# VectorE scales the turned x before ScalarE copies the turned B out of the same PSUM bank

## The reference, cut to what matters

```python
xBC = silu(causal_conv4(x @ Win_xBC.T))           # 256 columns of x, 128 of B, 128 of C
dtp = softplus(dt + dt_bias); dA = exp(dtp * A)   # 4 heads
def step(h, (dA_t, dt_t, x_t, B_t, C_t)):
    h = dA_t * h + (dt_t * x_t) outer B_t         # state 64 x 128 per head
    return h, C_t . h + D * x_t
y = rmsnorm(ys) * norm_w * silu(z) @ Wout.T
x = layernorm(x + y)
x = layernorm(x + two_of_eight_experts(x))        # gelu, 128 -> 512 -> 128
```

## Time and profile before

| | us |
|---|---|
| runs, median (three runs: 731.25, 731.27, 729.77) | 731.25 |
| profiled execution, its own time | 729.96 |
| span of the profiled execution | 728.2 |
| PE busy | 656.8 (90%) |
| DVE busy | 567.1 (78%) |
| ACT busy | 472.8 (65%) |
| POOL busy | 459.5 (63%) |

### The profile page before, as it was taken

How to read it: one execution, slowest core, us unless ns; L and a number is a source line. 1 busy time by engine, 2 the same in 40 slices (tenths; PEclk the granted TensorE clock), 3 DMA queues, 4 the chain that set the end, 5 groups by cost and what they waited for, 6 DMA issues and landing times.

```text
span 728.2 us, 19939 instructions
## 1 busy us (share of the span) xinstructions
PE 656.8 (90%) x5075; PEld 539.5 (74%) x5075; DVE 567.1 (78%) x1876; ACT 472.8 (65%) x1174; POOL 459.5 (63%) x664
## 2 busy tenths in 40 slices
PE   7978999999999999999999679999999999999910
PEld 5846756676666666756675569999999999999910
DVE  3478898999899999999999857677666666888744
ACT  3746767776777676767676527765656656677724
POOL 5022367777777776777677565767775455677754
PEclk9999999999999999999999999999999999999975
DMA  9180001101110111011101022332432223455443
GB/s 254 38 289 15 2 26 35 45 20 42 30 45 20 42 32 43 23 39 34 41 24 37 16 74 56 91 86 79 101 94 71 75 72 94 140 164 171 140 173 123
DMA packets 56543, 54.54 MB, mean 75 GB/s; under 512 B 9562, under 2 KB 45790, under 8 KB 56176
## 3 DMA queue, kind: packets, MB, share of 16 engines
q1 hardware_dynamic: 45712, 33.67, 16.9%
q0 software_dynamic: 8416, 16.93, 6.8%
q10 hardware_dynamic: 2304, 2.65, 1.0%
HBM read 31.05 MB, written 22.63 MB: 74 GB/s over the span
## 4 chain that ended last, share of the span: by engine, by line
PE 71%; DVE 9%; issue 8%; DMA 3%; POOL 3%; ACT 2%; SPq 1%; DVEq 1%; ACTq 0%; POOLq 0%
PE p L630 12%; PE pl L621 8%; PE pj L483 6%; PE p L682 4%; PE p L712 4%; PE p L621 4%; PE p L676 4%; PE p L720 3%; PE p L658 3%; PE p L691 2%; PE pj L491 2%; PE p L594 2%; PE p L580 2%; PE p L491 2%; PE pl L527 2%
## 5 line engine op out<-in xcount | busy, mean ns | idle before, releaser
L1651 POOL DMA_INDIRECT moe_rows<-xT x135 | 134.9, 999 | 79.6 <-DVE xT L1275 47.5
L1584 POOL DMA_INDIRECT sorted_rows<-pair,slot x128 | 128.6, 1004 | 32.5 <-issue 30.4
L1033 DVE SCALAR_TENSOR_TENSOR acc<-pj,conv_w_sb,acc 128x511 f32<-128x511 f32 (+2 forms) x192 | 142.3, 741 | 4.6 <-ACT acc L815 1.6
L630 PE MATMUL p<-w,xT 128*128 x1080 | 143.5, 276 | 1.6 <-ACT xT L950 1.3
L950 ACT ACTIVATE xT<-pl,b_sb 128x128 f32<-128x128 f32 x360 | 102.7, 369 | 47.5 <-PE pl L621 45.7
L630 PEld LDWEIGHTS p<-w,xT 128*128 128x128 f32 x1080 | 131.4, 192 | 2.8 <-issue 2.8
L621 PE MATMUL pl<-xT 128*128 128x128 f32 x720 | 95.1, 275 | 2.4 <-DVE xT L1263 2.4
L1271 DVE TENSOR_TENSOR xT<-p,b_sb 128x128 f32<-128x128 f32 x135 | 39.3, 291 | 64.5 <-PE p L630 60.6
L621 PEld LDWEIGHTS pl<-xT 128*128 128x128 f32 x720 | 87.5, 192 | 2.5 <-issue 2.5
L815 ACT ACTIVATE acc<-pj,conv_b_sb,conv_w_sb 128x512 f32<-128x512 f32 x64 | 49.5, 773 | 33.6 <-PE pj L483 33.6
L483 PE MATMUL pj<-xT,w_xbc 128*128 128x512 f32 x128 | 67.2, 607 | 0.0
(11 more groups left out here) (223 smaller groups left out, 1406.8 us busy)
## 6 DMA issues: line engine op xcount, KB each, us to landing
xT<-sorted_rows SPq DMA_DIRECT2D x135, 65.0 KB, 2.4
xres<-in_x SPq DMA_DIRECT2D x16, 256.0 KB, 3.0
w<-in_w SPq DMA_DIRECT2D x2, 2048.0 KB, 10.0
acc<-moe_rows SPq DMA_DIRECT2D x12, 256.0 KB, 3.8
xT<-moe_rows SPq DMA_DIRECT2D x12, 256.0 KB, 5.5
out<-sz ACTq DMA_DIRECT2D x10, 256.0 KB, 2.6
moe_rows<-xT POOLq DMA_INDIRECT x135, 2.3
sorted_rows<-pair,slot POOLq DMA_INDIRECT x128, 2.4
```

The source lines that it names most:

```text
L630: mm = pe.matmul(y_bank(j)[:, 0:P], hT[j % 4][:, f, :], w2[:, bass.ds(e, 1), f, :].rearrange("p e d -> p (e d)"), start=(f == 0), stop=(f ...
L1033: ins = dve.scalar_tensor_tensor(out=acc[:, k, j:TOKS], in0=pj[k % 2][:, 0:TOKS - j], scalar=conv_w[:, k, TAPS - 1 - j:TAPS - j], in1=acc[ ...
L1584: pool.indirect_dma_start(out=sorted_rows[:, :], out_offset=bass.IndirectOffsetOnAxis(slot[q.par][:, c, k:k + 1], 0), in_=(rowA, rowB)[k][ ...
L1651: pool.indirect_dma_start(out=moe_rows[:, :], out_offset=bass.IndirectOffsetOnAxis(xs[k][:, P:P + 1].bitcast(I32), 0), in_=ye[j % 8], in_o ...
```

## The change

It does three things. DVE no longer waits for `Btok_ready` ahead of `Xdt`: it needs only the turned rows. ACT's copy of the turned B waits for `Xdt_ready` of the same chunk where it waited for `tr_psum`, so that the order of the two readers of `p5` is turned round in chunks 0, 1 and 2. And in chunk 0 the exponential of chunk 1's exponents, with its table load, is issued ahead of the copy, where it was issued behind it; in the other chunks it stood ahead already. PE's and POOL's code is not touched: PE still waits for both `Xdt_ready` and `Btok_ready` before it overwrites `p5`.

```diff
                 for c in range(NC):
                     n = NC * s.n + c
-                    if scan and c > 0 and (c + 1 < NC or project):
+                    if scan and (c + 1 < NC or project):
                         exp_exponents(n + 1, c + 1)
                     if scan and c + 1 < NC:
-                        act.wait_ge(tr_psum, n + 1)
+                        act.wait_ge(Xdt_ready, n + 1)
                         wait(act, state_psum, (NC - 1) * s.n + c - 1)
                         act.copy(Btok[c % 2][:, :], p5[:, CC * P:(CC + 1) * P]).then_inc(Btok_ready, 1)
-                    if scan and c == 0:
-                        exp_exponents(n + 1, c + 1)
                     if not route and c == 0:
                         enter_dt(1, G0, SEQS)
...
                         dve.wait_ge(tr_psum, n + 1)
-                        if c + 1 < NC:
-                            dve.wait_ge(Btok_ready, (NC - 1) * s.n + c + 1)
                         wait(dve, Xdd_ready, (NC - 1) * s.n + max(c - 1, 0))
                         dve.tensor_tensor(heads(Xdt[c % 2][:, :]), heads(p5[:, 0:DI]),
                                           per_head(cur[s.par][:, 0, :], c), ALU.mult).then_inc(Xdt_ready, 1)
```

## The result

| | before | after |
|---|---|---|
| median of ten runs (lowest to highest), us | 730.14 (729.39 to 731.27) | 726.88 (724.77 to 729.07) |
| profiled execution, own time | 729.96 | 724.77 |
| its span | 728.2 | 723.0 |
| its granted clock, share of full speed | 0.976 | 0.979 |

The ratio of after to before is 0.9953, with an interval of 0.9942 to 0.9964: 3.4 us less, between 2.6 and 4.2. The forecast was 727.8 with "faster" at 0.74.

The account below looks back on a forecast made before the run. DVE's path to `state` in chunk 0 was taken as the bound, with PE's path 0.20 ahead of it. 13 x 0.21 + 0.52 + 2 x 0.1 = 3.45 us off the median 731.25 gave 727.8, range 725.5 to 730.9.

Parts of the forecast that it names:

- `Xdt` 0.35 earlier, the load right behind the SiLU, the copy 0.50 behind the exponential: Chunk 0: `Xdt` at 237.93, load at 237.42 without waiting, exponential 0.79 earlier, ACT's copy from 239.21 to 239.48.
- rival A: Chunk 0: the table load waits for PE's exponents, the 13 slots gain nothing, 730.7; chance 0.14.
- the drain of some 1380 ns: Extra cost at ACT's table switch; forecast took none, else copy 1.38 later, 16 us over all slots; one chance in a hundred.
- `yv` 0.35 earlier: Chunk 0, DVE's path: `yv` starts at 240.43, so DVE could take `state` at 240.76.
- POOL takes the gain of `Xdd`: Chunk 0: POOL's scatter runs until 238.79, so `Xdd` starts at 238.80 and ends hardly earlier.
- PE's exponents don't move, `state` waits for the product, 0.19 to 0.23 a slot: Chunk 0: chunk 2's exponents stay at 239.53 to 239.57, `state` at 240.88 to 240.92 instead of 241.11; 0.21 taken.
- Rival C: Chunk 0: DVE's path decides after all, the slot gains the full 0.35, 5.3 in all, 726.0; chance 0.06.
- Rival B: Chunk 0: ACT's copy later, exponents of chunk 2 near 239.9; up to 0.18 a slot slower, 733.1; chance 0.08 with drain.
- Chunks 1 and 2 of ordinary slots give nothing: PE wants the later copy over 0.9 after it lands in chunk 1; PE's projection sets chunk 2's pace; nothing gained or lost.
- Slot 15: Chunk 2, no projection: `Xdt` at 420.35 instead of 420.87, PE at 420.88 instead of 421.40; 0.52 gained into the second phase.
- Slots 0 and 1, a choice of 0.1 each: These slots have other work around them, softplus and decays; gain chosen as 0.1 each, half of the others'.
- The sum: Whole kernel: 13 x 0.21 + 0.52 + 2 x 0.1 = 3.45 us, from the median 731.25 to 727.8, 0.47% below.

Follow-up runs that it names:

- The delays: Changed kernel, chunk 0: unread 512-column ACT copy ahead of the `Btok` copy, 780.86, ratio 1.0039; unread 8-column DVE copy ahead of the statistics, 769.00, ratio 0.9951.
- the run with the exponents ahead: Changed kernel; PE's waits for `Btok` and `Xdd` in chunk 0 put behind chunk 2's exponents: 766.15, ratio 0.9899; again 765.54, ratio 0.9914.
- the two halves: New order in chunk 0 only on the changed kernel: 767.25, ratio 0.9910; new order in chunks 1 and 2 only on the kernel before: 773.36, ratio 1.0005.
- the version with `state` first: Changed kernel, chunk 0; PE issues the product of `Btok` and `Xdd` ahead of the exponents, DVE takes `state` ahead of `yv`: 770.39, ratio 0.9962.

## Why the prediction was right, and where it was not

- **`Xdt` 0.35 earlier, the load right behind the SiLU, the copy 0.50 behind the exponential.** Right to 0.01. The load started at 234.24, 0.01 behind the SiLU and ahead of the end of PE's exponents (233.99 + 0.38 = 234.37); rival A needed it at or behind that end, and is false. The exponential starts 0.01 behind the end of the load: the drain of some 1380 ns in the Trainium skill (ScalarE: Activation LUTs, What ACT_TABLE_LOAD costs) isn't there, its 1283 ns are.
- **`yv` 0.35 earlier.** It was 0.41. The forecast read DVE's path as free of gaps and saw the exponential only as a danger for later; it already held the mask for about 0.06. At `state` this makes no difference, for PE's path decides there.
- **POOL takes the gain of `Xdd`.** Right: `Xdd` starts 235.65, right behind the scatter (234.66 + 0.96 = 235.62).
- **PE's exponents don't move, `state` waits for the product, 0.19 to 0.23 a slot.** Right: 0.20, and no more because PE now waits for ACT's copy. The delays (0.50 paid in full on ACT, 0.07 hidden on DVE) and the exponents moved ahead on the changed kernel (0.15 gained) show that PE's wait for ACT is the limit now. That DVE's path was the limit before is read from the earlier trace rows, `state` 0.33 behind `yv` without a wait; the same move on the old kernel gave nothing, but shortened PE's path too little to decide it. Rival C, all of 0.35 by this change alone, is false: that needs PE's order changed too, as in the run with the exponents ahead.
- **Rival B** did not come about; its place is the right one, its point of decision was not reached (the copy was at 1.33, as worked out). Its sum doesn't come out either: 239.57 and the added 0.08 and 2 x 0.04 make 239.73, not 239.9, and so fall short of the 239.76 that it names itself.
- **Chunks 1 and 2 of ordinary slots give nothing.** Shown by the two halves.
- **Slot 15: the step that failed.** The forecast had 0.52 pass "straight through to the second phase". The slot, chunk 2, after:
```profile
414.61 0.27 PE L654 MATMUL p<-ident,xc 128*128 128x128 f32 x1
...
414.92 0.42 DVE L1309 TENSOR_TENSOR Xdt<-p,cur 128x256 f32<-128x256 f32 x1 [1.83 <-PE p L654]
...
415.14 1.08 POOL L1580 DMA_INDIRECT sorted_rows<-pair,slot  x1 [0.22 <-issue]
...
415.45 0.66 PE L676 MATMUL p<-M,Xdt 128*64 128x128 f32 x8
...
416.25 0.63 POOL L1593 TENSOR_TENSOR Xdd<-Xdt,cur 128x256 f32<-128x256 f32 x1
...
417.02 0.67 PE L691 MATMUL p<-Xdd,Btok 128*128 128x256 f32 x2 [0.27 <-POOL Xdd L1593]
...
419.34 0.66 PE L676 MATMUL p<-M,Xdt 128*64 128x128 f32 x8
```
And before, the rows that stand beside them and the earlier trace rows:
```profile
421.39 0.60 POOL L1597 TENSOR_TENSOR Xdd<-Xdt,cur 128x256 f32<-128x256 f32 x1 [0.57 <-DVE Xdt L1313]
...
424.78 0.66 PE L676 MATMUL p<-M,Xdt 128*64 128x128 f32 x8
```
The first half came: `Xdt` 0.04 behind the turn and PE 0.57 behind it, where it was 1.09. But a scatter of POOL runs from 415.14 to 416.22. Before, POOL had been idle for 0.57 when `Xdt` released `Xdd`; now `Xdd` waits for POOL, and the product for `Xdd`, 0.27. From the end of the turn to PE's products of chunk 3 it is 4.46 after (419.34 - 414.88) and 4.47 before: all is given back. I had asked this question of POOL in chunk 0 and not here.

The runs on the other chips bear it out. Counted from slot 15's `state` of chunk 0, and taking the kernel before and the changed one on chip 8, `Xdt` of chunk 2 starts at 7.62 and 7.10 and PE's products with `M` at 8.14 and 7.62, but `Xdd` at 8.43 and 8.44, behind the scatter in both (7.32 + 1.08 = 8.40), and PE's products of chunk 3 at 11.52 in both. With the new order in chunk 0 only these products are at 8.14 and 11.52, with it in chunks 1 and 2 only at 7.62 and 11.51: the 0.52 appears with the order of chunk 2 and is gone by chunk 3. That POOL's scatter is what takes it is read from the rows; no run moved the scatter.
- **Slots 0 and 1, a choice of 0.1 each.** 0.15 in slot 0; slot 1 can't be parted from the clock.
- **The sum.** 2.62 measured where 13 x 0.21 = 2.73 stood, and about 0.25 for slots 0 and 1, make 2.9 on the first chip; the forecast had 3.45, of which 0.52 did not exist. The measured 3.4 (2.6 to 4.2) doesn't tell the two apart, the traces do. The number itself, 727.8, came out 0.9 above the 726.88 measured because it stood on the median of three runs, 731.25; the ten runs give 730.14, and the same sum taken from there gives 726.7.

Open: the second phase. From the GELU's load to the end it took 332.6 to 335.4 us in the four profiles of chip 8, whose code for it is the same: about as much as the whole effect. In the traces of these chips ACT waits there for something that the profile calls remote, 41 to 54 us in all; in the first two profiles it doesn't. The ratio of 0.9910 for the order in chunk 0 only, with a first phase like the changed kernel's, is not explained; its profiled execution, 771.74, was the longest of the seven, so no trace shows a short one.

## What to carry to other kernels

Where two paths join, write down both ends: the gain of shortening one is the distance to the other (0.20 of 0.41 here), and the move that shortens the second (a wait put behind work that doesn't need it) gave 0.15 once the first was short and nothing before, where it had only some 0.1 to take. Ask of each engine that feeds the join what else stands in its queue, in every place where the change acts and not only in the one that repeats. Edits that look separable may each be a loss alone (+1.0% and +2.2%) and a gain together (-0.5%).

## What the runs showed of the hardware

- A table load that carries no wait of its own runs ahead of the wait of its exponential: 0.13 us before the exponents' end in slot 8. The first GELU's load still comes behind PE, with 8.18 us of idle time ahead of it, as in the earlier trace rows.
- The same program took 730 us in the first runs and 772 to 777 on chips 2, 8 and 11, at a mean granted clock of 0.976 in the first profile and 0.965 in that of chip 8. The first GELU's load is at 435.15 in the one and 437.82 in the other, so nearly all of it is in the second phase. The reason isn't known.
- In chunk 0 of slot 8, ACT's copy started 0.04 us behind the end of PE's turn on the first chip and 0.08 on another, and DVE's `Xdt` 0.04 behind it (after, first chip) and 0.14 (236.90 - 236.76, after, the other).
- A DVE sum of 128x4 (`gsum`) took 0.38 to 0.43 us in the 13 ordinary slots of the version with `state` first, where it starts while a POOL instruction of 0.60 runs, and 0.15 to 0.17 in the same slots of the kernels before and after, where it does not. The cause was not tested by itself.
